# Doubling the scale buffer, giving up the output buffer, and reordering mask and product units in a scan-as-blocks kernel

## The reference, cut to what matters

```
bc = einsum('bti,oi->bto', value, W_bc).reshape(B, T, H, 4, N)      # Bz, Bx, Cz, Cx
bc = bc / (sqrt(sum(bc * bc, axis=-1)) + EPS)
S = 1 / (1 + dt*k + dt*dt*A)
z = S * (z - dt*A*s + dt*(Bz * u))
s = s + dt*z + dt*(Bx * u)
y = einsum('bhn,bhnd->bhd', Cz, z) + einsum('bhn,bhnd->bhd', Cx, s)
```

## Time and profile before

| | |
|---|---|
| median of 3 runs | 2403.24 us (2394.12 to 2406.58) |
| profiled execution | 2401.71 us, its span 2400.0 us |
| mean granted clock of PE | 0.894 |
| busy PE, DVE, ACT, POOL | 2009.4, 1911.9, 932.8, 311.4 us |
| mixer, from its first to its last instruction | about 288 to 2107 us |
| phase, start of `coefficients` to the next | 102.7 to 114.3 us over the 14 between 473.3 and 1982.5 us |

### The profile page before, as it was taken

One profiled execution on the slowest core, in us unless ns is written; L12 is line 12 of the kernel. 1 busy time (PEld: TensorE's weight loads), 2 busy tenths in 40 slices (PEclk: granted clock), 3 DMA queues, 4 the chain that ended last, 5 costly groups with the idle time before them and its releaser, 6 DMA issues. The chain is left out here.

```text
span 2400.0 us, 73278 instructions
## 1 busy us (share of the span) xinstructions
PE 2009.4 (84%) x29474; PEld 1234.3 (51%) x29474; DVE 1911.9 (80%) x4411; ACT 932.8 (39%) x1913; POOL 311.4 (13%) x588
## 2 busy tenths in 40 slices
PE   5776294898999899898989898998989897828896
PEld 2333142465555555464555555465555556726775
DVE  5776445989798987978897898989798889538885
ACT  3555231343435333343435343343424342205554
POOL 0000111111121211111221111111121111000000
PEclk9888697899999999898999998899989996559999
DMA  3555653364544535344544545464545433073410
GB/s 95 165 174 166 164 140 95 101 157 115 134 134 138 139 111 145 114 125 124 151 118 130 148 123 130 114 153 113 134 134 135 127 108 93 14 216 138 169 64 27
DMA packets 231278, 304.40 MB, mean 127 GB/s; under 512 B 115744, under 2 KB 132128, under 8 KB 222752
## 3 DMA queue, kind: packets, MB, share of 16 engines
q1 hardware_dynamic: 123968, 148.65, 21.7%
q10 hardware_dynamic: 86368, 96.50, 14.1%
q0 software_dynamic: 20608, 54.56, 8.9%
HBM read 240.85 MB, written 57.68 MB: 124 GB/s over the span
## 5 line engine op out<-in xcount | busy, mean ns | idle before, releaser
L695 PE MATMUL m_ps_a<-m_valT,m_w_bc 128*128 128x512 f32 x2048 | 1011.8, 636 | 56.6 <-DMA m_valT<-scratch_valT 39.3
L695 PEld LDWEIGHTS m_ps_a<-m_valT,m_w_bc 128*128 128x128 f32 x2048 | 385.9, 200 | 455.5 <-issue 438.0
L644 POOL DMA_DIRECT2D m_shear<-scratch_shear x512 | 273.1, 534 | 1294.2 <-DVE m_psi L1020 1183.7
L834 ACT ACTIVATE m_sq<-m_ps_a 128x512 f32<-128x512 f32 x256 | 152.9, 597 | 548.5 <-PE m_ps_a L695 548.5
L1020 DVE TENSOR_TENSOR m_psi<-m_psi,m_prod 128x128 f32<-128x128 f32 x1024 | 295.5, 289 | 20.2
L1016 DVE TENSOR_TENSOR m_prod<-m_psi,m_shear 128x128 f32<-128x128 f32 x1024 | 292.6, 286 | 16.9 <-issue 1.1
L756 PE MATMUL m_ps_g<-m_raw 32*64 32x64 f32 x8192 | 177.8, 243 | 105.6 <-DVE m_g L1125 83.1
L756 PEld LDWEIGHTS m_ps_g<-m_raw 32*64 32x64 f32 x8192 | 157.4, 154 | 188.4 <-issue 183.9
L1080 DVE TENSOR_TENSOR m_part<-m_raw,m_psi 128x1024 f32<-128x1024 f32 x128 | 155.8, 1220 | 22.2 <-issue 21.2
L1043 DVE TENSOR_TENSOR m_raw<-m_raw,m_scale 128x1024 f32<-128x1024 f32 x64 | 78.2, 1223 | 114.5 <-DMA m_scale<-scratch_norm 112.4
L224 PE MATMUL ps_w<-p_xnT,w_in 128*128 128x512 f32 x256 | 129.8, 660 | 40.3 <-ACT vraw L282 34.9
(11 more groups left out here) (154 smaller groups left out, 2713.0 us busy)
## 6 DMA issues: line engine op xcount, KB each, us to landing
m_scale<-scratch_norm SPq DMA_DIRECT2D x512, 128.0 KB
m_w_bc<-in_w_bcT ACTq DMA_DIRECT2D x252, 256.0 KB, 3.5
m_shear<-scratch_shear POOLq DMA_DIRECT2D x512, 64.0 KB, 2.9
m_det<-scratch_ab POOLq DMA_DIRECT2D x64, 256.0 KB, 6.2
scratch_yT<-m_y ACTq DMA_DIRECT2D x64, 224.0 KB, 2.4
scratch_gateT<-gate SPq DMA_DIRECT2D x8, 1024.0 KB, 3.9
scratch_valT<-val SPq DMA_DIRECT2D x8, 1024.0 KB, 4.4
scratch_svgT<-svg SPq DMA_DIRECT2D x8, 1024.0 KB, 5.7
```

Of the source, the lines that this page charges most:

```text
L644: pool.dma_start(shear[h * N:(h + 1) * N, w % 2].rearrange("p k g t -> p k (g t)"), spread(src)).then_inc(into.sem, into.step)
L695: mm = pe.matmul(ps_a[j % 2].ap(), w_bc[:, j, kt, :], valT[:, kt, :], start=(kt == 0), stop=(kt == KI - 1))
L834: act.activation(sq[:, j, :], ps_a[j % 2].ap(), ACT.Square).then_inc(sq_ready.sem, sq_ready.step)
```

## The change

Buffers: `scale` gets a second slot, so that input and output scales no longer share one; the input load waits for the input scaling of the group before, the output load for its output scaling. `y` is gone: `copy_y` writes into the Cx part of `raw` of its own group, the store reads it there, and ACT's copy of a later Cx unit into that place waits for the store. `of_segment` (8 masks of 32 columns) becomes slices of one `band` of 39 columns, filled by one ACT operation in the place of 8.

Order of DVE: both scalings of a group stand together; the first mask stands before `coefficients` (it stood in the middle of `states`), the second before the third group's queries (it stood after them); the scalings of the second, third and fourth group of "next" come later. Order of PE: a product unit stands before `outputs` of the first and of the third group, where all stood after. ACT and SP follow.

```diff
-        scale = sb("scale", [P, 2, T])
+        scale = sb("scale", [P, 2, 2, T])
-        y = sb("y", [ROWS, T])
@@ SP: input_scales, output_scales
                     sp.wait_ge(rows_stored.sem, rows_stored.at(b, group))
-                    sp.wait_ge(c_scaled.sem, c_scaled.at(b, group - 1))
+                    sp.wait_ge(b_scaled.sem, b_scaled.at(b, group - 1))
                     load_scales(group % 2, 0)
...
-                    sp.wait_ge(b_scaled.sem, b_scaled.at(b, group))
+                    sp.wait_ge(c_scaled.sem, c_scaled.at(b, group - 1))
                     load_scales(group % 2, 1)
@@ SP: the body; load_valT now before norm_rows(b, then + 2)
+                            for i in range(2):
+                                norm_rows(b, then + i)
+                                input_scales(b, then + i)
+                                output_scales(b, then + i)
+                                if i == 0:
+                                    load_e_end(b, half + 1)
                         if half == 0 and not last:
                             load_valT(b + 1)
                         if more:
+                            for i in range(2, HALF):
+                                norm_rows(b, then + i)
+                                input_scales(b, then + i)
+                                output_scales(b, then + i)
@@ PE: the body
                             scores_and_unit(b, first + i, unit, last)
+                            unit += 1
+                            if i != 2:
+                                products(b, unit, 1, last)
+                                unit += 1
                             outputs(b, first + i - 1)
-                            products(b, unit + 1, 1, last)
-                            unit += 2
+                            if i == 2:
+                                products(b, unit, 1, last)
+                                unit += 1
@@ ACT: evacuate, copy_y, the body
                     act.wait_ge(y_made.sem, y_made.at(b, group - HG))
+                    if j == NJ - 1:
+                        stored = y_stored[group % HALF]
+                        act.wait_ge(stored.sem, stored.at(b, group // HALF - 2))
                     act.activation(raw[:, group % HG, j, :], ...
...
-                    act.wait_ge(y_stored.sem, y_stored.at(b, group - 1))
...
                         block_states(b, first)
-                        evacuated(1)
+                        evacuated(2)
                         copy_y(b, first)
                         block_states(b, first + 1)
                         store_y(b, first, more)
-                        evacuated(2)
+                        evacuated(1)
                         copy_y(b, first + 1)
...
-                        evacuated(1)
+                        evacuated(2)
                         copy_y(b, first + 2)
                         block_states(b, first + 3)
                         store_y(b, first + 2, more)
-                        evacuated(1)
                         copy_y(b, first + 3)
@@ DVE: phase
                     keys(b, first + 2, advance)
                     if more:
                         scale_inputs(b, then, advance)
+                        scale_outputs(b, then, advance)
                     det_sums(b, half, advance)
+                    keys(b, first + 3, advance)
                     if more:
-                        scale_outputs(b, then, advance)
                         scales(b, then + 1, advance)
-                    keys(b, first + 3, advance)
-                    queries(b, first, advance)
+                    queries(b, first + 0, advance)
+                    queries(b, first + 1, advance)
+                    mask(b, first + 0, advance)
+                    coefficients(b, half, advance)
+                    states(b, half, advance)
+                    mask(b, first + 1, advance)
+                    queries(b, first + 2, advance)
                     if more:
                         scale_inputs(b, then + 1, advance)
-                    queries(b, first + 1, advance)
+                        scale_outputs(b, then + 1, advance)
                     if more:
-                        scale_outputs(b, then + 1, advance)
                         scales(b, then + 2, advance)
-                    coefficients(b, half, advance)
-                    states(b, half, advance, lambda: mask(b, first, advance))
-                    if more:
-                        scale_inputs(b, then + 2, advance)
-                    queries(b, first + 2, advance)
-                    mask(b, first + 1, advance)
-                    if more:
-                        scale_outputs(b, then + 2, advance)
-                        scales(b, then + 3, advance)
                     queries(b, first + 3, advance)
                     mask(b, first + 2, advance)
                     if more:
-                        scale_inputs(b, then + 3, advance)
+                        scale_inputs(b, then + 2, advance)
+                        scale_outputs(b, then + 2, advance)
+                    if more:
+                        scales(b, then + 3, advance)
                     advance(OF_PHASE)
                     mask(b, first + 3, advance)
                     if more:
+                        scale_inputs(b, then + 3, advance)
                         scale_outputs(b, then + 3, advance)
                         keys(b, then, stepping(b, half + 2, not last))
```

More of the change, by code:

```diff
@@ L455, in mix @@
         head_sum = sb("head_sum", [P, N])
-        of_segment = sb("of_segment", [P, N // HP, N])
+        band = sb("band", [P, N // HP - 1 + N])
         causal = sb("causal", [P, C])
@@ L504, in mix @@
         rows_stored = sig("rows_stored", HG, 16)
[L505 removed]
+        scale_in = [sig(f"scale_in{n}", HG * HP, 16) for n in range(2)]
         a_made = sig("a_made", UNITS)
@@ L531, in mix @@
         y_ready = sig("y_ready", HG * 2)
-        y_stored = sig("y_stored", HG, 16)
+        y_stored = [sig(f"y_stored{s}", 2, 16) for s in range(HALF)]
         narrow_next = sem("narrow_next")
@@ L565, in load_scales @@
                         src = dram["norm"][slot].rearrange("(j h) t -> h j t", h=HP)[h, 2 * half:2 * half + 2]
-                        sp.dma_start(scale[h * N:(h + 1) * N, :, :], spread(src)).then_inc(scale_in.sem, scale_in.step)
+                        sp.dma_start(scale[h * N:(h + 1) * N, half, :, :], spread(src)).then_inc(scale_in[half].sem, scale_in[half].step)
                 def load_valT(b):
@@ L815, in _ @@
                 act.wait_ge(const_set, 7)
-                for s in range(N // HP):
-                    act.activation(of_segment[:, s, s::N // HP], head_sum[:, 0:HP], ACT.Copy).then_inc(segments_ready, 1)
+                act.activation(band[:, N // HP - 1::N // HP], head_sum[:, 0:HP], ACT.Copy).then_inc(band_ready, 1)
                 act.activation(A.ap(), A.ap(), ACT.Exp).then_inc(A_ready, 1)
@@ L887, in store_y @@
                     act.wait_ge(y_ready.sem, y_ready.at(b, group * 2 + 1))
-                    act.dma_start(dram["yT"][b, group, 0:ROWS, :], y.ap()).then_inc(y_stored.sem, y_stored.step)
+                    stored = y_stored[group % HALF]
+                    act.dma_start(dram["yT"][b, group, 0:ROWS, :], raw[0:ROWS, group, 3, :]).then_inc(stored.sem, stored.step)
                     if more:
@@ L956, in _ @@
                 over_rows(act, body)
-                act.wait_ge(y_stored.sem, y_stored.at(B - 1, HG - 1))
+                for stored in y_stored:
+                    act.wait_ge(stored.sem, stored.at(B - 1, 1))
             @block.vector
@@ L1040, in scale_inputs @@
                     dve.wait_ge(raw_ready.sem, raw_ready.at(b, group * NJ + 1))
-                    dve.wait_ge(scale_in.sem, scale_in.at(b, (group * 2 + 1) * HP - 1))
+                    dve.wait_ge(scale_in[0].sem, scale_in[0].at(b, (group + 1) * HP - 1))
                     v = raw[:, group % HG, 0:2, :]
-                    dve.tensor_tensor(v, v, scale.ap(), ALU.mult).then_inc(b_scaled.sem, b_scaled.step)
+                    dve.tensor_tensor(v, v, scale[:, 0], ALU.mult).then_inc(b_scaled.sem, b_scaled.step)
                     advance(ns(2 * T))
@@ L1048, in scale_outputs @@
                     dve.wait_ge(raw_ready.sem, raw_ready.at(b, group * NJ + 3))
-                    dve.wait_ge(scale_in.sem, scale_in.at(b, (group * 2 + 2) * HP - 1))
+                    dve.wait_ge(scale_in[1].sem, scale_in[1].at(b, (group + 1) * HP - 1))
                     v = raw[:, group % HG, 2:4, :]
-                    dve.tensor_tensor(v, v, scale.ap(), ALU.mult).then_inc(c_scaled.sem, c_scaled.step)
+                    dve.tensor_tensor(v, v, scale[:, 1], ALU.mult).then_inc(c_scaled.sem, c_scaled.step)
                     advance(ns(2 * T))
@@ L1146, in coefficients, with states @@
                         advance(ns(28))
-                def states(b, half, advance, between):
```

(1 more changed line is left out.)

30 lines of the change are left out of this document (7 added, 23 removed).

## The result

The changed kernel takes 2539.27 us (median of 4 runs, 2528.81 to 2545.77) against 2402.12 for the kernel before (4 runs, 2394.12 to 2406.58). The ratio is 1.0571, 95% interval 1.0521 to 1.062: slower by 137 us. The profiled execution took 2545.77 us, its span is 2544.1 us. The forecast was 2525.

A forecast was written before the change was run, and what follows sets the result against it. The prediction took DVE's fixed work and waits to bound the kernel. Scales +93 us (88 in 14 phases, 5 in the last row), first mask +49 and first groups -14 make 128 on 2401.7: 2530, said 2525, range 2425 to 2610.

The forecast's parts named there:

- DVE paces: A phase of 107.8 us is DVE's 94.4 us of fixed work, its waits and 3.5 us of small gaps.
- The scales, +88 us in 14 phases: DVE's waits for scales at the scalings: 14.7 us a phase against 8.4, +6.3 us in each of 14 phases.
- the third input: Third group's input scaling, its load beside the determinant load: waits 3.3 us a phase (bounds 0.8 to 5.3).
- the fourth input: Fourth group's input scaling, with 3.8 us of cover against 8.3 us: waits 4.5 us a phase (3.1 to 6.5).
- the fourth output: Fourth group's output scaling, with 1.1 us of cover: waits 1.6 us a phase (0 to 2.9).
- the two other output terms: Output scaling waits of the first group, 1.0 us (0 to 2.9), and the third, 1.3 us (0 to 3), a phase.
- The output set close behind the input set: Output scale loads: by the skill they land 1.2 us behind, all three output waits go, the sum is 55 us lower.
- The first mask, +49: DVE's first mask waits for PE's first scores: 5.5 us in first halves of rows, 1.5 in second, seven each.
- The first four groups, -14: Output scaling waits of the first four groups fall from 18.9 us to 4 x 1.2: -14 us.
- PE's changes hide: PE's moved units (3.6 us each) lie in its waiting time; PE can afford 2 to 4 us once a row.
- Rival 1: The scalings lack a buffer: all scale waits go, 117 us and 43 us of the first groups; 2291 us, chance 0.04.
- Rival 2: PE paces: 66.9 us of its waits for the first mask go, giving 2321 us; chance 0.05.

The follow-up runs named there:

- e1: The changed kernel with DVE's scalings and scale rows back in the old order, SP's value load behind the third group's scales: 2432.16 us, ratio 1.012.
- e3: The changed kernel with POOL's determinant load cut to a quarter of its size after the first phase, for timing alone: 2491.24 us, ratio 1.0384.
- e6: The changed kernel with the four determinant sums moved in front of the first group's input and output scalings: 2440.96 us, ratio 1.0167.
- e2: The changed kernel with the first mask back among the state steps and the second behind the third group's queries: 2502.15 us, ratio 1.042.
- e5: The changed kernel with DVE's whole old order, SP's value load behind the third group's scales; buffers and other orders stay changed: 2412.12 us, ratio 1.0034.
- e4: The kernel before with all buffer changes (second scale slot, y in raw, band) and no order changes: 2392.97 us, ratio 0.9958.
- e7: e6 with the second to fourth group's scalings put where enough work lies before them, and the value load as in e1: 2413.41 us, ratio 1.0029.
- e8: e4 with the determinant sums in front of the first input scaling and the fourth input scaling behind the last mask: 2368.24 us, ratio 0.9878.
- e10: The kernel before with the determinant sums before the first input scaling and the first output scaling behind the fourth keys: 2385.47 us, ratio 0.9918.

## Why the prediction was right, by its own steps

1. *DVE paces: 94.4 us of work and its waits.* Held for the change: 94.6 us a phase, and the new waits (143.6 us) make up the stretch's growth (140.2).
2. *The scales, +88 us in 14 phases.* Measured +100.5. The mean input waits a phase of the four groups, over the 14 phases: 3.2, 0, 4.1, 4.9 us (predicted 3.0, 0, 3.3, 4.5), one wait of 4.1 us for `raw` among them; output waits 0.5, 0, 0.9, 2.4 us (predicted 1.0, 0, 1.3, 1.6). The mechanisms are shown by undoing them: e1 (all four places), e3 (the determinant load), e6 (the first group's cover). The terms that were too small are the third input (0.8 us), the fourth input (0.4) and the fourth output (0.8), 28 us over 14 phases, of which the two other output terms gave back 13. The fourth output's bounds went up to 2.9 us by a second set that takes 2.4 us to move; no run shows that figure, they show only the waits.
3. *The output set close behind the input set.* By the Trainium skill (DMA: Bandwidth & Descriptors, anatomy of one DMA) I had worked out that these three waits go. The page gives that fit for DMAs that GpSimd issues, and these are issued by SP, which I had not said. Measured the waits are 0.5 + 0.9 + 2.4 = 3.8 us a phase, against the 3.9 taken from the rows of before. The measurement decides here: the second set did not land in time for a scaling that could start 2.1 us behind the first (first and third group) or 1.2 us (fourth).
4. *The first mask, +49.* Measured 43.1 us in the 14 phases and 7.5 in the one before them. It is 5.6 to 7.9 us in the first halves of the seven rows that the loop runs, 0.4 in that of the unrolled last row, and 0 to 1.5 in second halves (predicted 5.5 in all first and 1.5 in all second ones; the term was 5.9 us too high). The chain from the last sum to the second part of the scores took 27.6 to 29.9 us in the first halves of the seven (predicted 28.8), 22.5 in the last row's, and 21.4 to 23.5 in second ones (21.5); DVE needed 21.9 us to the end of the second queries in nearly all of them (21.8). e2 gives 37 us back for it.
5. *The first four groups, -14.* The output waits gave 15.3, but the input waits there, which I had left as they were, took back 3.9, and the first mask took 7.5, which I had not counted there. The stretch ahead of the 14 phases became 5.1 us shorter and not 14.
6. *PE's changes hide.* In the changed kernel the new waits of DVE make up the growth without them, so they seem to; no run has the changed kernel with PE's old order. As a price of "nothing", put without a bound, it was wrong outside of it: e5 against e4 shows 19 us for the orders of PE, ACT and SP where DVE's order is the old one. The wait that took the place of PE's 66.9 us, 106.2 us for the key copies, was not sized either.
7. *Rival 1* (the buffer): scale waits rose, and e4 shows 10 us for all buffers in the place of 117. *Rival 2* (PE paces): 66.9 us of PE's waits went and phases grew by 10.0 us. It was wrong as a forecast of this change, but PE is close behind: without the scale waits DVE waits for PE and ACT instead (e1, e7). The prediction's model of a phase, DVE's work plus its waits, tells what added waits cost; it can't tell what removed waits bring. I used it that way in the expectations of e1 and e4, and both came out too low, by 67 and 28 us.
8. *The total.* It is closer than its terms. In the 14 phases the scales were 12.5 us too low and the mask 5.9 too high; ahead of them the sum was 8.9 us too low and behind them 4.0. The range of 2425 to 2610 is not what its text says: the forecast's own bounds give 2401.7 - 42 - 14 = 2345 us to 2401.7 + 239 + 84 - 14 = 2711. The range was a choice inside them.

Left open: how much of PE's longer busy time (98.3 to 102.9 us for the same matmuls) is a cause and how much a consequence. Busy time times clock is 92.5 to 94.5 us a phase in every row of the table, so the busy time follows the clock. The clock was lowest (0.90) in the changed kernel, where PE is idle longest (15.0 us a phase), but e1 has 7.4 us of idle time and 0.91, e8 6.6 us and 0.95. No experiment held the clock fixed.

## What to carry to other kernels

- When work stands between the start of a DMA round trip and its use, it is cover: count it in microseconds against the measured round trip (here 6.3 to 11.2 us alone in the kernels before and after, 10.3 to 15.9 beside a 1 MB load) for each place, before and after the move. A second buffer is worth something only where the first was still in use when the load could have started; added to the order of before it brought 10 us (e4). In an order that covers the trip it may bring more, but e8 against e10 (17 us by the medians) doesn't show it: their intervals overlap, and they also differ in the place of the fourth input scaling and the first output scaling.
- A model in which one engine's waits add up prices additions well and removals badly. Before a gain is promised, look at the busy time of the next engine, here PE's 98 to 103 us. No order tried here left PE idle for less than 6.6 us a phase, and part of that was PE waiting for DVE.
- Put the head of the longest chain through other engines (here the determinant sums, to ACT, PE and back to DVE) before any wait: one line moved was worth 98 us in the changed kernel.

## What the runs showed of the hardware that was not expected

- Eight DMAs of 128 KB in one go take SP 3.94 and 4.31 us to issue in the two sets shown, against 1.71 for four. In the mean the second four hold the output scaling, which could start 2.1 us behind the first one, by 0.5 us in the first group and by 0.9 beside the 1 MB load; in the fourth group it could start 1.2 us behind and is held by 2.4.
- With a 1 MB load from POOL's queue, issued some 2 us behind the scale rows, the round trip of a small store and four loads took 13.6 us in the mean; with a load of a quarter of that it took 9.5 or less (e3).
- In first halves PE stops twice, in the state terms and in the first scores, with nothing shown that it waits for: 1.88 and 1.60 us at 922.31 and 937.36 us, and 1.2 to 2.4 us each time in all seven rows that the loop over rows runs. In the last row, which is unrolled, the first scores run through and the state terms stop for 0.93 us. The kernel before has the same stops in the same seven rows (1.5 to 2.6 us in the first scores, 0.5 to 2.4 in the state terms) and none in the last. The longer chain for which the mask waits contains them; in the changed kernel it is some 6 us shorter in the last row and in second halves. So the stops go with the looped code; what they are was not looked for.
